# GpSimd's dt times u in the second layer's mixers, given to VectorE in slots of its own

## The reference, cut to what matters

```
xi = silu(causal_depthwise_conv(x @ Win_x, convw, convb))     # u, 512 channels
dt = softplus(xi @ Wx_dt @ Wdt + bdt)                          # 512 channels
h[t] = exp(dt[t] * A) * h[t-1] + (dt[t] * u[t]) * B[t]         # 16 states for each channel
y[t] = sum over the states of h[t] * C[t], plus u[t] * D
out  = (y * silu(z)) @ Wout
```

## Time and profile before

| | |
|---|---|
| median of 3 runs | 3668.19 us (3656.0 to 3673.11) |
| the profiled execution's own time | 3672.47 us |
| its span, first to last instruction | 3670.8 us |
| mean granted clock of TensorE over the span | 0.916 of full speed |
| the stretch of the second layer's scans | 1111 to 3134 us of the span |

### The profile page before, as it was taken

One profiled execution on the slowest core, in us unless ns is written; L12 is line 12 of the kernel. 1 busy time (PEld: TensorE's weight loads), 2 busy tenths in 40 slices (PEclk: granted clock), 3 DMA queues, 4 the chain that ended last, 5 costly groups with the idle time before them and its releaser, 6 DMA issues. The chain is left out here.

```text
span 3670.8 us, 27563 instructions
## 1 busy us (share of the span) xinstructions
PE 2889.5 (79%) x7494; PEld 1196.8 (33%) x7494; DVE 2834.1 (77%) x2237; ACT 1881.2 (51%) x2469; POOL 2287.1 (62%) x1102
## 2 busy tenths in 40 slices
PE   5677677767556879788898888798897887579998
PEld 2222222344222333333333333233333332244443
DVE  4899799433238999999999999999999999462222
ACT  4575576434245555555555655555555554352222
POOL 2598399100116989889889899898899898100000
PEclk7799699899777999999989999999899999889999
DMA  1011011153714444554555455555445555201110
GB/s 58 16 51 47 7 52 50 35 183 114 245 52 153 158 172 172 166 183 168 168 179 172 157 182 177 165 172 174 169 162 181 179 178 200 83 23 34 34 34 11
DMA packets 163606, 451.10 MB, mean 123 GB/s; under 512 B 23328, under 2 KB 52192, under 8 KB 163456
## 3 DMA queue, kind: packets, MB, share of 16 engines
q1 hardware_dynamic: 156576, 424.60, 34.5%
q0 software_dynamic: 6912, 25.17, 1.7%
HBM read 414.85 MB, written 34.87 MB: 123 GB/s over the span
## 5 line engine op out<-in xcount | busy, mean ns | idle before, releaser
L1317 POOL TENSOR_TENSOR mix_prod<-mix_spread,mix_h 128x1024 f32<-128x1024 f32 x512 | 1374.4, 2686 | 247.4 <-DVE mix_h L1723 131.4
L1817 PE MATMUL mix_banks<-mix_prod,kept_ident 128*128 128x512 f32 x2048 | 1049.6, 638 | 80.9 <-POOL mix_prod L1317 54.1
L1367 ACT ACTIVATE mix_side_in<-mix_dt,mix_neg_a 128x1024 f32<-128x1024 f32 x384 | 437.7, 1141 | 315.6 <-DVE mix_h L1723 312.2
L1817 PEld LDWEIGHTS mix_banks<-mix_prod,kept_ident 128*128 128x128 f32 x2048 | 406.1, 202 | 515.8 <-issue 302.9
L1709 DVE TENSOR_TENSOR mix_banks<-mix_banks,mix_dtu 128x1024 f32<-128x1024 f32 x384 | 467.1, 1216 | 10.0 <-PE mix_banks L1807 5.9
L1723 DVE TENSOR_TENSOR_SCAN mix_h<-mix_side_in,mix_state,mix_banks 128x1024 f32<-128x1024 f32 x192 | 450.6, 2347 | 18.1 <-issue 0.4
L1807 PE MATMUL mix_banks<-mix_parts,kept_sel 96*128 96x512 bf16 x768 | 250.0, 410 | 260.5 <-DVE mix_h L1723 252.4
L1723 DVE TENSOR_TENSOR_SCAN mix_h<-mix_side_in,mix_banks 128x1024 f32<-128x1024 f32 x192 | 438.8, 2286 | 18.9 <-ACT mix_side_in L1367 1.3
L1327 POOL TENSOR_TENSOR mix_side_in<-mix_spread,mix_dtu 128x512 f32<-128x512 f32 x256 | 339.0, 1324 | 0.1
L2053 POOL DMA_DIRECT2D out<-finb_o x8 | 5.8, 728 | 525.0 <-DVE finb_eps L2192 525.0
L435 POOL TENSOR_TENSOR mix_drive<-mix_drive,mix_du 128x1024 f32<-128x1024 f32 x128 | 305.2, 2400 | 40.5 <-ACT mix_drive L500 40.3
(11 more groups left out here) (264 smaller groups left out, 4499.4 us busy)
## 6 DMA issues: line engine op xcount, KB each, us to landing
mix_spread<-c_rows SPq DMA_DIRECT2D x640, 512.0 KB, 3.9
mix_c_row<-c_rows SPq DMA_DIRECT2D x40, 512.0 KB, 3.6
exa_f<-f SPq DMA_DIRECT2D x32, 512.0 KB, 4.8
slot_outputs<-exa_inter POOLq DMA_DIRECT2D x32, 512.0 KB, 3.9
ln_zp<-slot_outputs SPq DMA_DIRECT2D x8, 2048.0 KB, 10.2
first_acc<-xT SPq DMA_DIRECT2D x8, 512.0 KB, 4.1
x_scratch<-first_acc POOLq DMA_DIRECT2D x8, 512.0 KB, 4.0
fw_scratch<-mix_res SPq DMA_DIRECT2D x8, 512.0 KB, 6.3
```

The costliest lines, as they stand in the source:

```text
L1317: pool.tensor_tensor(prod[:, un % 2, :], spread[:, i % SLOTS, :], h[:, un % HR, :], ALU.mult).then_inc(prod_ready, 1)
L1367: act.activation(drive[un % 2] if pooled(un) else side_in[:, un % 2, :], dt[:, at // NS, :], ACT.Exp, scale=neg_a[:, way(p), at:at + 1]).t ...
L1817: mm = pe.matmul(y_bank[:, hf, :], k.ident[:], half(prod[:, un % 2, :], hf), start=False, stop=True, skip_group_check=True)
```

## The change

The product dt * u of each block moves from GpSimd to VectorE: one instruction of 128 x 1024 in place of two of 128 x 512. It stands in slots 9, 22 and 27 of its pass for blocks 1, 2 and 3, and in slot 60 of the pass before for block 0, where the first half stood. GpSimd keeps nothing in its place. The waits (`soft_done`, `u_ready`) and the count of `dtu_ready`, one for each block, are the same.

```
         @block.gpsimd
-            def times_u(p, g, hf):
-                pool.wait_ge(soft_done, p * MB + g + 1)
-                pool.wait_ge(u_ready, p * MB + g + 1)
-                ins = pool.tensor_tensor(half(dtu[:, g, :], hf), half(dt[:, g, :], hf), half(u[:, p % 2, g, :], hf), ALU.mult)
-                if hf:
-                    ins.then_inc(dtu_ready, 1)
...
-            def side(p, s):
-                for g, at in ((1, (10, 14)), (2, (18, 22)), (3, (30, 34))):
-                    if 0 <= p < NP and s in at:
-                        times_u(p, g, at.index(s))
-                if p + 1 < NP and s in (60, 62):
-                    times_u(p + 1, 0, (60, 62).index(s))
...
-                    side(p, s)
         @block.vector
+            def times_u(p, g):
+                dve.wait_ge(soft_done, p * MB + g + 1)
+                dve.wait_ge(u_ready, p * MB + g + 1)
+                dve.tensor_tensor(dtu[:, g, :], dt[:, g, :], u[:, p % 2, g, :], ALU.mult).then_inc(dtu_ready, 1)
...
+                for g, s0 in ((1, 9), (2, 22), (3, 27)):
+                    if own and s == s0:
+                        times_u(p, g)
+                if ahead and s == 60:
+                    times_u(p + 1, 0)
```

## The result

The changed kernel takes 3691.71 us in the median of 7 runs (3677.37 to 3695.11), the kernel before 3664.84 in the median of 7 on the same chip: ratio 1.0069, 95% interval 1.0047 to 1.0091. In a second series it was 3686.11 us against 3667.87, ratio 1.0051, interval 1.0035 to 1.0068. The forecast was 3685 us and 1.0047: slower, by about the half per cent that I had called the limit of what can be told. It is told: both intervals lie above 1.

The account below looks back on a forecast made before the run. VectorE was taken to bound the scan stage. 34.7 + 1.3 - 6.5 - 1.3 - 1.3 - 2 - 6.6 - 1.1 = +17.2 us gave 3685 us, 0.47% slower, range 3668 to 3706.

Parts of the forecast that it names:

- What bounds the stage: Scan stage: VectorE, busy 97%, sets the pace; 81 us of work taken from GpSimd are worth nothing by themselves.
- steps (+34.7): Slots 9, 22, 27, 60: 31 new VectorE instructions, each lengthening the full queue by 1.12 us, +34.7 us.
- pass 0 (+1.3): Slots 9 and 22 of pass 0: the new instruction waits for GpSimd's half drive still running, +1.3 us.
- cover in slot 28 (-6.6): Block 3's new instruction in slot 27 replaces VectorE's wait for ScalarE's layernorm root chain in seven passes, -6.6 us.
- slot 15: Soft's second instruction no longer meets GpSimd's half product in six of eight passes, 1.1 us each, -6.5 us.
- slot 14, pass 0: One soft instruction of 5.6 us gets shorter once GpSimd's last half product is gone, -2 us.
- dtu waits: Pass starts: the wait before the very first drive shrinks, -1.3 us, and three others go, -1.3 us.
- cover of the first tap, ahead of slot 29: Pass 0: VectorE's 2.0 us wait for the first tap hides one more new instruction, -1.1 us.
- The product's mean: GpSimd's products: held up behind new instructions by 0.9 us each, their mean time rises by about 0.05 us.
- The turn is lost: Rival: at slots 9 and 22 GpSimd comes first, +36 us, 3704 us, half of it 3695; chance 0.16.
- No covers: Rival: ScalarE's chain moves too and slot 15's soft instruction stays long, +30 us, 3698 us; chance 0.14.
- More relief: Rival: long soft instructions in slots 5, 6, 14, 58 go too, -6 us, 3662; chance 0.12 half or third, 0.03 all.

## Why the prediction was right, point by point

**What bounds the stage.** Right. 31 new instructions of a step of 1.1 us each, on an engine that was busy for 97%, lengthened the stage, and the 81 us of work taken from GpSimd brought it 76 us more of waiting in front of its products.

**The sum, by slots.** Growth against the first profile of before, counted from the timelines of the two profiles of the changed kernel, in us:

```
term                                      predicted      first    second
steps (+34.7), pass 0 (+1.3),
  cover in slot 28 (-6.6)                   +29.4        +29.4    +29.4    slots 9, 22, 27, 60
slot 15                                      -6.5         -6.6     -6.6
slot 14, pass 0                              -2.0         -2.5     -2.5
dtu waits                                    -2.6         -2.9     -2.9    ahead of slot 0, slot 63
cover of the first tap, ahead of slot 29     -1.1         +0.3     +0.3
slot 11, pass 0                              not seen     +2.2     +2.2
```

The stage as a whole grew by 14.1 and 16.0 us where 17.2 stood. The rows of the table add up to 19.9, so the other slots, of which the forecast says nothing, were shorter by 5.8 and 3.9 us in sum. That the sum came out so near is in part luck, although its large terms are right one by one.

The 1.3 us of pass 0 came out as 1.4, but not as forecast. In slot 9, where a half drive was to have 0.71 us left, nothing was lost, since that half drive now starts 0.04 us behind the new instruction. In slot 22 the turn was lost, the only time: a whole product was running, and the new instruction takes 2.57 us. The product's mean rose by 23 ns where I expected 50.

**Two small terms that failed.** Both failed in pass 0, and by TensorE's clock. The wait of 2.0 us for the first tap did not shrink, it is 2.2 now. The chain in front of the tap starts on TensorE behind the scan of slot 26 and goes on to ScalarE. From TensorE's start to the tap it took 7.60 us in the first profile of before and 9.00 in both profiles of the changed kernel: 1.40 us more, against the 1.12 that the new instruction covers. All of it lies in TensorE's part, 5.60 us before and 7.00 after. These are the two halves of TensorE's part in the kernel before, and then in the changed one; the granted clock is the third number from the end:

```profile
1222.03:1225.75 3.72, 3.72 (x7) 1.67 (x7) 3.63 (x3) 2.46 (x4) 2.35 (x1) 0.57 0.37 130
1225.75:1227.60 1.85, 1.85 (x6) 0.76 (x5) 1.85 (x1) 0.00 (x0) 1.51 (x1) 1.00 0.58 224
```
```profile
1230.09:1234.34 4.25, 4.25 (x7) 1.79 (x8) 4.25 (x3) 2.18 (x4) 3.24 (x1) 0.50 0.31 112
1234.34:1236.93 2.59, 2.59 (x6) 0.97 (x4) 2.42 (x2) 0.29 (x1) 2.22 (x1) 0.66 0.58 201
```

The cover itself works: with block 3 alone on VectorE the chain took 7.74 us and the wait fell to 1.0. And the wait was not a fixed price: in the second profile of before the clock was 1.00 over TensorE's part, the chain took 6.05 us and the wait 0.4.

The other term is slot 11. Slot 11 of pass 0 grew by 2.2 us: VectorE waited 2.1 us for TensorE, the longest of the seven waits shown above. TensorE's four matmuls of block 2's dt took 3.78 us there:

```profile
1160.27 3.11 PE L1812 MATMUL mix_banks<-mix_prod,kept_ident 128*128 128x512 f32 x4 [2.22 <-POOL mix_prod L1310]
1163.32 3.78 PE L1771 MATMUL mix_banks<-mix_rows,mix_wdt 16*128 16x512 f32 x4
```

In the kernel before the same four took 1.98 us. The windows of the two stretches, the changed kernel first, the one before second:

```profile
1163.40:1167.00 3.60, 3.60 (x4) 1.07 (x4) 2.59 (x2) 2.51 (x4) 2.70 (x2) 0.50 1.01 349
```
```profile
1155.50:1157.40 1.90, 1.90 (x5) 0.62 (x4) 1.90 (x1) 0.00 (x0) 1.90 (x2) 1.00 0.82 313
```

Half clock is 1.2 of 2.4 GHz; ahead of it TensorE had waited 2.22 us for a product of GpSimd's, where it had waited 0.61 in the kernel before. Both profiles of the changed kernel show the same. I had said that TensorE's `add` comes later, but so does VectorE, and left its clock out. Each of the two places is in pass 0 alone; in sum they are 3.6 us that the forecast lacked.

**The term that was read from one execution.** The forecast's six times 1.1 us in slot 15 and its -2 us in slot 14 are right against the first profile of before, and that profile was not a typical one. In the second, four and not six of the instructions of slot 15 are long, that of slot 14 in pass 0 takes 2.11 us and not 5.62, and slots 55 and 58 are 4.6 us shorter; its stage is 2011.1 us, 13 less. Against the mean of both, 2017.5, the changed kernel's stage, 2039.0 in the mean of its two, is 21.5 us longer. That is where the difference between the forecast of 17 us and the two measured ones, 27 and 18 between the medians, can come from; the intervals, which overlap, don't require more. The run with the product left out (-14 us) plus the 29.4 us of the four slots gives +15, under both; that the two simply add is assumed. I also expected the mean of line 1604 to fall by about 200 ns from 1719. It fell by 173 and 63 in the two profiles, and in the second profile of before, with nothing changed, it was 1538.

**The rivals.** The turn is lost: but for that one time it wasn't, the new instruction's median is 1.20 us, but the run with the instruction behind the drive shows that its price was of the right size: 1.09 us in the slot, 20 to 27 us in the kernel. No covers: wrong, the wait went, and came back with the instruction one slot later. More relief: wrong; the long cases of slots 5, 6 and 58 were there without GpSimd's halves too, and lines 1599 and 1604 lost 10.1 and 5.9 us in sum against the first profile of before, under the 12 that would have spoken for it. In this rival's sum a step is off: -6 us and the 10.0 us of waits for TensorE make -16, which is not yet faster than 0.5%. The rule of the Trainium skill ("SBUF — State Buffer", section Who interferes with whom) that whichever comes second is blocked until the first has finished its whole instruction, agrees with the product of 3.25 us behind the new instruction and with the 2.49 us of the new one behind a product. The turns that GpSimd kept over several instructions are shown by the runs alone.

## What to carry to other kernels

Before work is moved to the engine that sets the pace, count its steps, then look at each place for two things: a wait right behind it that the instruction can replace (eight instructions cost 2 us in front of such a wait, and 12 us more one slot later), and what GpSimd is doing at that moment. As these runs show it, on VectorE beside a busy GpSimd an instruction with two SBUF inputs belongs at the very start of the stretch that frees GpSimd's next work: 0.17 us ahead of that work it costs 1.1 us (slot 9), 0.4 us behind it 2.9 (slot 17). And the size of a relief that hangs on a race should be taken from more than one profile.

## What the runs showed that I had not expected

VectorE's instruction can be passed over: it waited for three of GpSimd's, 5.62 and 5.16 us, though only one was running when it came. This was seen once in the first profile of before and three times in slot 14 with the halves moved (passes 0, 2 and 6), each time with more work of GpSimd ready; twice in slot 15, with block 2's soft instructions moved there, it waited for two products (3.93 and 3.96 us). What decides it is open. And the stage of one kernel, some 2020 us, differed by 13 us between two profiles, for the most part from a handful of meetings of VectorE and GpSimd that went one way or the other; 1.6 us of it is the wait for the first tap.
